# Four jobs of a state-space scan moved between engines: skip term, normalisation, end decay, state sum

## The reference

```python
xn = (x - mu) * rsqrt(var + 1e-5) * ln_w + ln_b          # over channels
z, xBC, dt = split(einsum('bchw,dc->bdhw', xn, in_proj_w))
xBC = silu(conv3x3_depthwise(xBC) + conv_b)              # 256 + 32 + 32 channels
dt = softplus(dt + dt_bias);  A = -exp(A_log)            # 8 heads of 32
# chunks of q = 128 positions; Acs = cumsum(dt * A) in a chunk
Ldec     = where(tri, exp(Acs[i] - Acs[j]), 0)
Y_diag   = (C B^T * Ldec) @ (xs * dt)
states   = B^T @ (exp(Acs[-1] - Acs) * xs * dt)          # the end decay
S[c+1]   = exp(Acs[-1]) * S[c] + states[c]
Y_off    = exp(Acs) * (C @ S[c])
y = Y_diag + Y_off + D * xs                              # the skip term
y = y * silu(z);  y = y * rsqrt(mean(y*y) + 1e-5) * rms_w
x = x + y @ out_proj_w^T
```

## Time and profile before

| | us |
|---|---|
| median of 3 runs (2485.59 to 2492.06) | 2489.66 |
| the profiled execution | 2490.13 |
| its span, first to last instruction | 2488.4 |
| the scan with chunks, first L891 to last t drain | 90.2 to 740.6 |

### The profile page before, as it was taken

The page is one execution under the profiler, slowest core; times in us unless marked ns, Lnnn a source line. Parts: engine busy times, 40 slices in busy tenths (PEclk is TensorE's granted clock), DMA queues, the critical chain, the costliest instruction groups (busy, mean ns, idle before and its releaser), DMA issues. The chain is left out here.

```text
span 2488.4 us, 41622 instructions
## 1 busy us (share of the span) xinstructions
PE 2235.4 (90%) x12035; PEld 1803.0 (72%) x12035; DVE 1699.6 (68%) x4560; ACT 1279.2 (51%) x2815; POOL 1635.1 (66%) x1774
## 2 busy tenths in 40 slices
PE   4798898899886999999999999999999997499994
PEld 2466666666664888888888888888888886388883
DVE  5787987888745667767767777677777775244444
ACT  3454554554532666666666666666666664133331
POOL 2688878887861666576685776766757766355551
PEclk9887887787876999999999999999999998699996
DMA  2930000000000001010010010100100100355555
GB/s 89 387 128 9 9 9 1 9 1 1 18 5 23 1 2 24 2 30 13 7 36 1 12 31 4 37 4 8 35 2 12 31 4 30 129 194 189 197 180 203
DMA packets 135413, 131.05 MB, mean 53 GB/s; under 512 B 82885, under 2 KB 101359, under 8 KB 135190
## 3 DMA queue, kind: packets, MB, share of 16 engines
q1 hardware_dynamic: 124950, 107.12, 14.1%
q0 software_dynamic: 9088, 17.07, 2.0%
q10 hardware_dynamic: 1152, 4.19, 0.4%
HBM read 64.78 MB, written 65.10 MB: 52 GB/s over the span
## 5 line engine op out<-in xcount | busy, mean ns | idle before, releaser
L1191 POOL TENSOR_TENSOR plo<-pf,phi 128x512 fp32r<-128x512 f32 (+3 forms) x768 | 775.3, 1018 | 414.5 <-ACT phi L1414 385.3
L1412 ACT ACTIVATE pf<-psum 128x512 f32<-128x512 f32 (+3 forms) x768 | 379.3, 494 | 479.1 <-PE psum L1252 339.1
L1414 ACT ACTIVATE phi<-psum 128x512 fp32r<-128x512 f32 (+3 forms) x768 | 377.1, 491 | 0.0
L1301 PE MATMUL psum<-xT,qT 128*128 128x512 f32 (+3 forms) x768 | 286.1, 372 | 43.9 <-DVE nmax L1557 30.2
L1557 DVE CUSTOM_DVE_ANT_0 masked<-psum,ahead_wide 128x128 f32<-128x128 f32 (+3 forms) x512 | 248.2, 485 | 66.9 <-PE psum L1301 60.2
L1250 PE MATMUL psum<-phi,x_tok 128*128 128x512 f32 (+3 forms) x768 | 289.0, 376 | 0.8 <-POOL plo L1191 0.8
L1252 PE MATMUL psum<-qT,xT 128*128 128x512 f32 (+3 forms) x768 | 266.5, 347 | 0.0
L1251 PE MATMUL psum<-qT,xT 128*128 128x512 f32 (+3 forms) x768 | 266.1, 347 | 0.0
L1250 PE MATMUL psum<-qT,xT 128*128 128x512 f32 (+3 forms) x768 | 265.7, 346 | 0.0
L1251 PE MATMUL psum<-plo,x_tok 128*128 128x512 f32 (+3 forms) x768 | 265.0, 345 | 0.0
L1252 PE MATMUL psum<-phi,x_tok 128*128 128x512 f32 (+3 forms) x768 | 265.0, 345 | 0.0
(11 more groups left out here) (288 smaller groups left out, 5324.5 us busy)
## 6 DMA issues: line engine op xcount, KB each, us to landing
wg<-turned_w SPq DMA_DIRECT2D x39, 874.0 KB
routed<-empty SPq DMA_DIRECT2D x1, 34056.0 KB, 95.7
xg<-routed SPq DMA_DIRECT2D x39, 264.0 KB
qT<-nmax SPq DMA_DIRECT2D x512, 0.5 KB
y<-chosen SPq DMA_DIRECT2D x8, 1024.0 KB, 10.3
turned_w<-wT SPq DMA_DIRECT2D x8, 874.0 KB
x_in_sb<-in_x SPq DMA_DIRECT2D x8, 512.0 KB, 3.3
out<-o_st ACTq DMA_DIRECT2D x8, 512.0 KB, 5.2
```

What stands on the lines that cost most here:

```text
L1191: g_.tensor_tensor(plo[:, T % RP, 0:n], pf[:, T % RP, 0:n], phi[:, T % RP, 0:n].bitcast(F32), ALU.subtract).then_inc(a["low_ready"], 1)
L1301: t.matmul(bank[3][:, 0:n], qT[:, g % 2, 0, i * P:(i + 1) * P], xT[:, b % 2, 0, k0:k0 + n], start=True, stop=True).then_inc(a["peak_ready" ...
L1412: s_.activation(pf[:, T % RP, 0:n], bank[T % RS][:, 0:n], ACT.Exp)
L1414: s_.activation(phi[:, T % RP, 0:n], bank[T % RS][:, 0:n], ACT.Exp).then_inc(a["high_ready"], 1)
```

## The change

Four jobs change engines in the scan.
- Skip term: `dx`, its product and its sum on GpSimd go. `skip_w`, made once on VectorE, is the identity with D on its diagonal (128x128 for each half of the heads). TensorE multiplies the turned xs by it into bank 4, as the first matmul of a group of four heads, whose matmuls then accumulate.
- Normalisation: ScalarE does it, as rstd x t + shift, in slot 6 between its decays and its copy of the turned rows; GpSimd makes shift = -mean x rstd in `deviation`, two more operations.
- End decay: VectorE copies only the last column of Ldec to `to_end` (128x8). GpSimd makes `Xd` a step later, as `chunk_end(step - 1)`, ahead of the next `xdt`. VectorE's chunk_in no longer waits for xdt.
- State: TensorE adds `faded` in bank 5 by a matmul with the identity, behind the chunk's own state; it waits there for `s_faded`. ScalarE copies the bank to S, behind its tok copy, as `state(step - 2)`.
- The buffer of xs is now read until y is made: SyncE's wait ahead of the Wu load and GpSimd's in silu_x go by `y_ready`.

```diff
-                    sp.wait_ge(s["tok_ready"], (B - 1) * NC)
+                    sp.wait_ge(s["y_ready"], (B - 1) * NC)
...
                         g_.tensor_tensor(rstd[:, :], mvx[:, :, 1], epst[:, 0:1].to_broadcast([P, NC]), ALU.add).then_inc(s["vx_ready"], 1)
-                        pool.wait_ge(s["vx_ready"], n + 1)
+                        g_.tensor_tensor(shift[:, :], mvx[:, :, 0], minus[:, 0:1].to_broadcast([P, NC]), ALU.mult).then_inc(s["vx_ready"], 1)
+                        pool.wait_ge(s["vx_ready"], 2 * (n + 1))
...
+                        pool.wait_ge(s["rstd_ready"], n + 1)
+                        g_.tensor_tensor(shift[:, :], shift[:, :], rstd[:, :], ALU.mult).then_inc(s["shift_ready"], 1)
...
-                        need(pool, "yd_ready", g - 3)
-                        g_.tensor_tensor(dx[:, g % 4, :].rearrange("p (h d) -> p h d", d=HD), xs3,
-                                         dvec[:, :].unsqueeze(2).to_broadcast([P, NH, HD]), ALU.mult).then_inc(s["dx_ready"], 1)
+
+                    def chunk_end(g):
+                        pool.wait_ge(s["to_end_ready"], g + 1)
+                        pool.wait_ge(s["xdt_ready"], g + 1)
+                        need(pool, "st_ready", g - 1)
+                        g_.tensor_tensor(Xd[:, g % 2, :].rearrange("p (h d) -> p h d", d=HD),
+                                         xdt[:, g % 2, :].rearrange("p (h d) -> p h d", d=HD),
+                                         to_end[:, g % 4, :].unsqueeze(2).to_broadcast([P, NH, HD]), ALU.mult).then_inc(s["xd_ready"], 1)
...
                         pool.wait_ge(s["y_drained"], g + 1)
-                        pool.wait_ge(s["dx_ready"], g + 1)
-                        g_.tensor_tensor(y1[:, g % 4, :], y1[:, g % 4, :], dx[:, g % 4, :], ALU.add).then_inc(s["yd_ready"], 1)
-                        pool.wait_ge(s["yd_ready"], g + 1)
...
                             chunk_rs(step - 3)
+                        if 0 <= step - 1 < G:
+                            chunk_end(step - 1)
                         if 0 <= step < G:
                             chunk_in(step)
...
-                        t.matmul(bank[5][0:NS, 0:DI], tok[:, g % 4, DI:DI + NS], Xd[:, g % 2, :], start=True, stop=True
-                                 ).then_inc(s["st_ready"], 1)
+                        last = t.matmul(bank[5][0:NS, 0:DI], tok[:, g % 4, DI:DI + NS], Xd[:, g % 2, :], start=True, stop=(c == 0))
+                        if c:
+                            pe.wait_ge(s["s_faded"], g - g // NC)
+                            last = t.matmul(bank[5][0:NS, 0:DI], ident[0:NS, 0:NS], faded[:, :], start=False, stop=True)
+                        last.then_inc(s["st_ready"], 1)
...
                         for h in range(NH):
+                            if h % 4 == 0:
+                                m = h // 4
+                                t.matmul(bank[4][:, DI + m * P:DI + (m + 1) * P], xsC[:, n % 2, m, sl], skip_w[:, m, :], start=True, stop=False)
                             last = t.matmul(bank[4][:, DI + h * HD:DI + (h + 1) * HD], Ldec[:, g % 2, h, :],
-                                            xdt[:, g % 2, h * HD:(h + 1) * HD], start=True, stop=True)
+                                            xdt[:, g % 2, h * HD:(h + 1) * HD], start=False, stop=(h % 4 == 3))
...
+                    def normalise(n, hf):
+                        act.wait_ge(s["shift_ready"], n + 1)
+                        need(act, "tb_ready", 2 * (n - 1) + hf + 1)
+                        for c in range(4 * hf, 4 * hf + 4):
+                            last = a_.activation(xt[:, c, :], t_all[:, n * NC + c, :], ACT.Identity, scale=rstd[:, c:c + 1],
+                                                 bias=shift[:, c:c + 1])
+                        last.then_inc(s["xt_ready"], 1)
...
+                    def state(g):
+                        act.wait_ge(s["st_ready"], g + 1)
+                        n, nn, j = front(g + 1)
+                        if has(n) and j in (0, 3):
+                            act.wait_ge(s["nacs_ready" if j else "dtabs_ready"], n + 1)
+                        need(act, "y_ready", g)
+                        need(act, "s_faded", g - g // NC)
+                        a_.activation(S[:, (g + 1) % 2, :], bank[5][0:NS, 0:DI], ACT.Copy).then_inc(s["state_ready"], 1)
...
                             if j == 6:
+                                normalise(nn, 0)
+                                normalise(nn, 1)
                                 turned_back(nn, 0)
...
                         dve.wait_ge(s["decay_ready"], g + 1)
-                        dve.wait_ge(s["tok_copied"], g + 1)
-                        dve.wait_ge(s["xdt_ready"], g + 1)
-                        need(dve, "st_ready", g - 1)
-                        v.tensor_tensor(Xd[:, g % 2, :].rearrange("p (h d) -> p h d", d=HD),
-                                        xdt[:, g % 2, :].rearrange("p (h d) -> p h d", d=HD),
-                                        Ldec[:, g % 2, :, P - 1:P].to_broadcast([P, NH, HD]), ALU.mult).then_inc(s["xd_ready"], 1)
-                        dve.wait_ge(s["xd_ready"], g + 1)
+                        dve.wait_ge(s["tok_ready"], g + 1)
+                        need(dve, "xd_ready", g - 3)
+                        v.tensor_copy(to_end[:, g % 4, :], Ldec[:, g % 2, :, P - 1]).then_inc(s["to_end_ready"], 1)
+                        dve.wait_ge(s["to_end_ready"], g + 1)
...
-                            v.tensor_copy(S[:, (g + 1) % 2, :], bank[5][0:NS, 0:DI]).then_inc(s["state_ready"], 1)
...
-                            dve.wait_ge(s["s_faded"], g - g // NC)
-                            v.tensor_tensor(S[:, (g + 1) % 2, :], faded[:, :], bank[5][0:NS, 0:DI], ALU.add).then_inc(s["state_ready"], 1)
...
-                        if has(nn) and j == 6:
-                            normalise(nn, 0)
-                            normalise(nn, 1)
```

More of the change, by code:

```diff
@@ L163, in hybrid_kernel @@
             xdt = sb1("xdt", [P, 2, DI])
-            dx = sb1("dx", [P, 4, DI])
+            skip_w = sb1("skip_w", [P, 2, P])
+            to_end = sb1("to_end", [P, 4, NH])
+            shift = sb1("shift", [P, NC])
+            minus = sb1("minus", [P, 1])
             Xd = sb1("Xd", [P, 2, DI])
@@ L184, in hybrid_kernel @@
                 conv_done tap_scaled tap_added th_made th_ready xs_ready thc_made thc_ready bcs_ready bc_ready resid_T resid_ready
-                tok_ready tok_copied seg_ready decay_ready gl_ready xd_ready xdt_ready dx_ready st_ready state_ready y_ready y_drained
-                yd_ready yg_ready ssq_ready ms_ready rs_ready b6_ready yT_copied t_ready t_drained mv_ready ve_ready rs2_ready lnx_ready
+                tok_ready tok_copied seg_ready decay_ready gl_ready xd_ready xdt_ready st_ready state_ready y_ready y_drained
+                to_end_ready shift_ready yg_ready ssq_ready ms_ready rs_ready b6_ready yT_copied t_ready t_drained mv_ready ve_ready rs2_ready lnx_ready
                 xnT_copied dve_step pool_step pad_zero s_faded edec_ready sums_apart chooser""".split()
@@ L248, in _ @@
                     g_.memset(ones_col[:, :], 1.0).then_inc(s["pool_step"], 1)
+                    g_.memset(minus[:, :], -1.0).then_inc(s["pool_step"], 1)
                     g_.memset(epst[:, :], EPS).then_inc(s["pool_step"], 1)
-                    pool.wait_ge(s["pool_step"], 8)
+                    pool.wait_ge(s["pool_step"], 9)
                     for m in (ident, ident_bf):
@@ L300, in silu_x @@
                         pool.wait_ge(s["th_ready"], 2 * n + m + 1)
-                        need(pool, "tok_ready", (n - 1) * NC)
+                        need(pool, "y_ready", (n - 1) * NC)
                         g_.tensor_tensor(xsC[:, n % 2, m, :].rearrange("p (h w) -> p h w", w=WW),
@@ L676, in chunk_in @@
                         need(act, "st_ready", g - 3)
-                        need(act, "dx_ready", g - 3)
                         need(act, "xdt_ready", g - 3)
@@ L712, in _ @@
                             chunk_in(step)
+                        if 0 <= step - 2 < G:
+                            state(step - 2)
                         if 3 <= step < G + 6:
@@ L796, in _ @@
                                          of_four[:, :].unsqueeze(1).to_broadcast([P, 2 * NC, 4]), ALU.mult))
+                    for m in range(2):
+                        link(v.tensor_tensor(skip_w[:, m, :].rearrange("p (h d) -> p h d", d=HD), ident[:, :].rearrange("p (h d) -> p h d", d=HD),
+                                             dvec[:, 4 * m:4 * m + 4].unsqueeze(2).to_broadcast([P, 4, HD]), ALU.mult))
                     dve.wait_ge(a_exp, 1)
@@ L804, in statistics @@
                         dve.wait_ge(s["resid_ready"], 2 * n + hf + 1)
-                        need(dve, "vx_ready", n)
+                        need(dve, "vx_ready", 2 * n)
                         for c in range(4 * hf, 4 * hf + 4):
@@ L813, in statistics @@
```

(9 more changed lines are left out.)

## The result

| | median, us | runs | lowest to highest | ratio to before, 95% interval |
|---|---|---|---|---|
| before | 2487.62 | 4 | 2481.24 to 2492.06 | |
| after | 2567.91 | 4 | 2564.27 to 2572.46 | 1.0326 [1.0296, 1.0355] |

The forecast was 2468 us, range 2432 to 2502. The kernel is 80 us slower, outside the range and on the other side. The span of the profiled execution grew from 2488.4 to 2566.6 us.

A forecast was written before the change was run, and what follows sets the result against it. VectorE and TensorE taking turns bound the loop, TensorE alone the last image. Rounds fall from 86.4 to 81.6 us, -31 us over about 6.5; +9 in the last image; net -22 on 2490.1 gives 2468 us, range 2432 to 2502.

The forecast's parts named there:

- The round of 81.6 us: Eight-step scan round: 76.6 us at full clock plus 5 us put back for half clock, against 86.4 before.
- I charge up to 1 us in slot 5: Slot (step modulo 8) 5: TensorE's second state matmul waits up to 1 us for GpSimd's faded; other slots nothing.
- TensorE's 2.8 us: TensorE's turn, segments, out-projection and first state matmul in a bare slot take 2.8 us; 3.7 with a projection.
- a chain through GpSimd of 2.4 to 4.5: From TensorE's tok_ready to faded: tok copy 0.4, xdt 0.6 to 1.7, gate 0.7 to 1.7, fade 0.65 us.
- Rival (c): Gains and losses cancel: the wait on faded costs 1 us in most slots, 3 us a round more; 2487 us; chance 0.18.
- I put back 5 us of the 8.7: Slots 6 and 7: half clock throughout would add 8.7 us to TensorE's share; 5 us charged a round.
- The two other gaps (ahead of slots 3 and 5): TensorE's idle gaps ahead of slots 3 and 5 mostly close, since VectorE is earlier and TensorE later.
- +9 us: Last image, bound by TensorE alone: each of eight steps takes 1.15 us longer, +9 us.
- gap of 2.3 us in slot 6: Slot 6: TensorE idles 2.3 us before it can turn xt, which ScalarE now normalises.
- (b): Slower: TensorE at half clock in slots 6 and 7, slow stretch in slot 1; 88.7 us a round, 2514 us; chance 0.20.

The follow-up runs named there:

- before_load: Kernel before plus overwritten matmuls: a 32x256 ahead of each state matmul from an image's second chunk, a 128x128 ahead of each four y matmuls; 2538.66 us, 1.0196.
- state_wait: Kernel before with TensorE waiting for faded between the state matmul and the y matmuls, no work added; 2534.59 us, 1.0196.
- state_load: Kernel before plus one overwritten 32x256 matmul with 32x32 weight ahead of each state matmul, no wait; 2528.97 us, 1.0163.
- state_load_wide: Kernel before plus one overwritten 256-column matmul with 128x128 weight ahead of each state matmul; 2492.35 us, 1.0015.
- after_y_first: Whole change with skip term, y matmuls and C x S ahead of the state matmuls and the wait for faded; 2501.93 us, 1.0071.
- after_filler: Whole change plus one overwritten 256-column matmul with 128x128 weight a chunk, ahead of the state's; 2545.5 us, 1.0266.
- skip_load: Kernel before plus an overwritten 128x128 matmul ahead of each group of four y matmuls, GpSimd keeping dx and its sum; 2480.05 us, 0.9992.
- p_skip: Kernel before with only the skip term moved to TensorE, dx and its sum leaving GpSimd; 2456.33 us, 0.9892.
- p_norm: Kernel before with only the normalisation moved to ScalarE; 2511.58 us, 1.0112.

## Why the prediction was wrong

**What held.** VectorE's 60 and GpSimd's 63 us (61, and 61 to 63), ScalarE's 50 (50), TensorE's own work of 71 (65 to 72), and that TensorE's waits for the drain would go from 7.3 us in a round to under 3 (3.3 us in the whole scan). Of the single prices, Xd on GpSimd was put at 1.14 us and took 0.85 in the round shown; the state copy 0.40 and 0.36; the ScalarE normalise 0.27 and 0.49, off by 1.7 us a round; VectorE's copy of the last column 0.2 and 0.36. None of these moves the sum by 80 us.

**Where the sum went wrong.** The round of 81.6 us with 71 us of own work left 10.6 us for idle time and for what half clock costs. The runs, in means over the five rounds of steps 10 to 49 (the last column is the length less the two before it):

| kernel | length | own work | idle | lost to half clock |
|---|---|---|---|---|
| forecast | 81.6 | 71 | 10.6 together | |
| before | 86.4 | 61.5 | 8.8 | 16.2 |
| after | 94.1 | 68.8 | 5.9 | 19.4 |
| before_load | 92.1 | 69.0 | 6.6 | 16.5 |
| state_wait | 90.8 | 61.5 | 9.8 | 19.5 |
| state_load | 90.3 | 65.2 | 4.7 | 20.4 |
| state_load_wide | 85.6 | 65.1 | 7.4 | 13.1 |
| after_y_first | 87.3 | 67.5 | 3.6 | 16.2 |

The own work was put high, if anything. What failed is that 25 us of lost time would become 10.6: they stayed at 25.3. Two steps of the prediction stand behind it.

**First step that failed: "I charge up to 1 us in slot 5, where the accC adds delay GpSimd, and otherwise nothing."** TensorE's 2.8 us were set against a chain through GpSimd of 2.4 to 4.5, and I took the lower end as the rule. But faded is late in 25 chunks of 56 (the weight load's wait, 30.2 us), up to 3.1 us, and the fade itself took 1.06 us a piece in the round shown, where I had 0.65. The wait itself came to 16.4 us in 11 times, where about 6.5 were charged; what it does to the others costs more. state_wait shows it in the kernel before: 50 us with nothing else changed, for 1.0 us more of idle a round. It stands ahead of y, for which VectorE waits, and half-clock time is 37 to 44 us. Within the change after_y_first is the counter-test: 66 us back for the order, of which the wait is a part. Rival (c) had this mechanism, at 3 us a round and 20 us in all.

**Second step that failed, and the larger one in a round (with y first, 19.8 us are still lost): "I put back 5 us of the 8.7. The two other gaps (ahead of slots 3 and 5) mostly close."** They did close, and idle fell from 8.3-10.0 to 4.4-7.3 us. The clock did not follow: 31 to 51 us of half clock a round, where those 5 us of added time meant 10. I took idle time to be the only thing that brings the clock down. Here it also falls in stretches in which TensorE is busy throughout, as at 464 us, behind the 128x8 projections (L439) and the 32-wide state matmuls. The trace of before had said so already, in the very round that I read:

```profile
372.00:379.00 7.00, 7.00 (x44) 5.31 (x43) 5.23 (x9) 5.92 (x13) 6.78 (x7) 1.00 0.00 0
379.00:380.00 1.00, 1.00 (x5) 0.71 (x5) 0.97 (x2) 0.97 (x2) 0.92 (x2) 0.62 0.00 0
380.00:381.00 1.00, 0.18 (x1) 0.00 (x0) 1.00 (x3) 0.97 (x4) 1.00 (x3) 0.50 0.03 8
...
419.00:427.00 8.00, 8.00 (x52) 6.28 (x51) 7.82 (x8) 2.93 (x8) 7.48 (x8) 1.00 0.00 0
427.00:428.00 1.00, 1.00 (x2) 0.23 (x1) 0.93 (x5) 0.00 (x0) 0.56 (x2) 0.51 0.00 0
```

At 379 us the gap comes behind the fall and not ahead of it, and at 427 there is none. Of the 33 falls of before between 120 and 820 us, 13 have TensorE busy through the eight microseconds ahead of them. (The ends of matmuls are modelled, so very short gaps can be hidden.) So closing gaps could not be counted on to give the clock back.

That an added narrow matmul costs by the clock and a wide one does not is shown by one pair, state_load against state_load_wide, 44 us against 4, on the kernel before; after_filler agrees within the change, less cleanly. With wide matmuls beside the narrow one, in before_load, the clock was as before. What brought the clock down at 464, 379 and 427 us is only inferred from what stands ahead of it.

The Trainium skill (TensorE: Matmul & The Clock Gate, "HAM oscillation — how this bites in real kernels") tells of idle gaps between bursts that send the clock to half, and of keeping the engine fed. Half of that agrees: skip_load adds work and has 20 us at half clock instead of 34 to 41. The other half does not: state_load adds work too, has about the smallest idle of the kernels made from before (4.4 to 4.9 us) and the longest half-clock time (41 to 48), and the falls above come with no gap ahead of them. The measurement decides: being busy was not enough here.

**The last image.** I put +9 us, eight times 1.15 at a clock of 0.96. Its eight steps became 12.2 us longer, and with the steps that drain the pipeline 15.2. Over the eight steps the clock is 0.84 against 0.90 before, and TensorE has no gap in them (0.6 us before). In p_skip, with the skip term's matmuls alone, three of its steps take 6.63 to 6.64 us, 0.44 more than the 6.20 of before.

**The normalisation.** I named the gap of 2.3 us in slot 6 (up to 2.8 measured) and saw in it only what it left of an existing stall. Alone the part costs 23 us; the drain's wait (47.5 us in p_norm, 47.0 before) does not go with it, and 9.7 us of the loss lie ahead of step 8.

**The rivals.** (b), 2514 us, is nearest, and right in that TensorE at half clock pays double for what it is given. Its place, slots 6, 7 and 1, and its cause, the gap at xt, answer to the normalisation's part, 23 to 28 us. The failure common to all my cases is that I priced four parts as one sum. One is a gain (-32 us), one nothing, two are losses, and the largest loss, the state with 82 us, has two causes that alone cost 44 and 50 us on the kernel before. Of these the sum held the matmul's own time and 1 us a round for the wait.

**What stays open.** Alone the parts are -32, +82, +23 to +28 and +5, together about 80, the loss of the whole. That is a coincidence as far as the runs show, for each costs something else in company: the state part 82 alone, 115 within the change and 24 in the order with y first. How much of state_wait's 50 us is its own idle time and how much comes by the clock was not separated, nor the wait from the order in after_y_first's 66. Of the 14.5 us ahead of step 8 the normalisation alone has 9.7 and the state part 5.5, while without the state part 3.5 are left and with y first 3.3; why they are lost was not looked into. Why skip_load gains as much clock as its work costs, while the equally wide state_load_wide gains less, is open, and so is why before_load costs 53 us when its two halves cost 44 and none.

## What to carry to other kernels

Where TensorE shares a loop with other engines and its granted clock is below 0.9, look at the shape of an added matmul: on this kernel, added alone, 128x128 weights were free (0 and +4 us), and 32x32 weights cost 44 us for 31 us of work. Read the clock before you explain it: look for falls with no gap ahead of them, and for gaps that come behind a fall. Put a matmul that waits for a slow engine behind those for which other engines wait: the same work in that order gave 66 us back. Take a bundle of moves apart before you judge it: two of these four, alone together, are 1.6% faster than before (the skip term alone 1.1%), all four 3.3% slower.

## What the runs showed of the hardware

- The granted clock can fall without an idle gap ahead of it. In after it is 1.00 at 463 us, 0.54 and 0.50 in the next two, TensorE busy 1.00 in each; in before it falls at 379 and 427 us; in state_load it is 0.73 over 56 gapless microseconds.
- A 32x256 matmul with a 32x32 weight takes about as long as a 128x256 one with a 128x128 weight (410 and 420 ns in the mean), but added to the same place the kernel with it has 41 to 48 us of half clock a round, with the other 24 to 34.
- Work can be added without its time: skip_load has 4.3 us more of own work a round than before and the same time (0.9992 [0.9968, 1.0015]), at 20 us of half clock a round instead of 34 to 41. after_filler has 0.5 us more a chunk than the change and is not slower, 1.0266 [1.0202, 1.033] against 1.0326 [1.0296, 1.0355].
- A wait that adds no work cost 50 us in state_wait, with 1.0 us more of idle time a round.
- ScalarE's 128x128 activation from a tile in SBUF with scale and bias took 486 ns, its copy from a bank 272.
